# Two attention layers and a mixture of experts: the last token tile taken first, dispatch from slot numbers, combine weights by ScalarE, combine by halves

## The reference

```python
x = x + xattn(layernorm(x), ctx, ctx, mask, ...)      # 16 heads, softmax over 257 context rows
x = x + attn(layernorm(x), W_Q, W_K, W_V, W_O)        # 16 heads, rotary angles, causal, 32 tokens
# mixture of experts on xn = layernorm(x) as 8 groups (G) of 128 tokens (S), 8 experts (E), C = 32
logits = einsum('GSM,ME->GSE', xn, router_w)
raw = softmax(logits); idx1 = argmax(raw); gate1 = raw at idx1; idx2, gate2: the same without idx1
p1 = place of the token in the queue of expert idx1; p2 = place in that of idx2, behind all first choices
combine[g,s,e,c] = gate1*(e==idx1)*(c==p1)*(p1<C) + gate2*(e==idx2)*(c==p2)*(p2<C)
dispatch = (combine != 0)
expert_inputs = einsum('GSEC,GSM->EGCM', dispatch, xn)
hidden = gelu(expert_inputs @ w0) * (expert_inputs @ w1)          # width 1368
out = einsum('EGCM,GSEC->GSM', hidden @ wo, combine)
x = x + out
```

## Time and profile before

| | us |
|---|---|
| median of 3 runs | 539.1 (538.63 to 541.59) |
| the profiled execution's own time | 542.8 |
| its span, first to last instruction | 541.0 |
| TensorE busy | 495.8 (92%) |
| VectorE busy | 394.0 (73%) |
| ScalarE busy | 324.6 (60%) |
| GpSimd busy | 256.6 (47%) |

### The profile page before, as it was taken

The page is one execution under the profiler, slowest core; times in us unless marked ns, Lnnn a source line. Parts: engine busy times, 40 slices in busy tenths (PEclk is TensorE's granted clock), DMA queues, the critical chain, the costliest instruction groups (busy, mean ns, idle before and its releaser), DMA issues.

```text
span 541.0 us, 18283 instructions
## 1 busy us (share of the span) xinstructions
PE 495.8 (92%) x6637; PEld 456.4 (84%) x6637; DVE 394.0 (73%) x1007; ACT 324.6 (60%) x839; POOL 256.6 (47%) x343
## 2 busy tenths in 40 slices
PE   1898999998999999999996578999999999999996
...
DVE  2545555676676667677687867789999999999963
...
PEclk9979999999999999999997665899999999999998
...
GB/s 171 187 74 88 26 42 40 43 42 23 42 22 39 39 28 31 39 39 2 3 5 310 3 1 1 118 197 154 162 231 176 188 145 197 171 160 217 80 1 78
DMA packets 58126, 48.92 MB, mean 90 GB/s; under 512 B 20942, under 2 KB 49744, under 8 KB 58064
## 3 DMA queue, kind: packets, MB, share of 16 engines
...
HBM read 46.86 MB, written 1.08 MB: 89 GB/s over the span
## 4 chain that ended last, share of the span: by engine, by line
PE 81%; issue 6%; ACT 4%; DVE 3%; DMA 3%; SPq 1%; POOL 1%; ACTq 0%; DVEq 0%; POOLq 0%
PE bank L225 20%; PE bank L227 18%; PE bank L226 18%; PE bank L638 5%; PE bank L606 3%; PE bank L659 3%; PE bank L563 2%; ACT Pr L1094 2%; PE bank L1024 2%; DMA w_raw<-in_L_xattn_Wk 2%; PE bank L913 2%; PE bank L795 1%; DMA last_prob<-Pr 1%; PE bank L766 1%; PE bank L755 1%
## 5 line engine op out<-in xcount | busy, mean ns | idle before, releaser
L225 PE MATMUL bank<-XT_lo,W_hi 128*128 128x256 f32 (+1 forms) x352 | 100.5, 286 | 1.4 <-ACT XT_lo L1282 1.4
L226 PE MATMUL bank<-XT_hi,W_lo 128*128 128x256 f32 (+1 forms) x352 | 100.1, 284 | 0.0
L227 PE MATMUL bank<-XT_hi,W_hi 128*128 128x256 f32 (+1 forms) x352 | 99.8, 284 | 0.0
L2275 POOL TENSOR_TENSOR W_lo<-raw,W_hi 128x256 fp32r<-128x256 f32 (+1 forms) x88 | 87.7, 996 | 7.0
L2190 POOL TENSOR_TENSOR Pr<-Pr,rinv 128x1028 f32<-128x1028 f32 (+2 forms) x32 | 60.5, 1890 | 49.6 <-DVE rinv L1441 48.9
L1094 ACT ACTIVATE Pr<-Sc,nmax 128x257 f32<-128x257 f32 x128 | 63.8, 501 | 22.2 <-DVE nmax L1430 19.5
L1430 DVE CUSTOM_DVE_ANT_0 Sc<-bank,mask_add 128x257 f32<-128x257 f32 x128 | 47.0, 423 | 40.0 <-PE bank L606 17.3
L1922 DVE TENSOR_TENSOR W_lo<-raw,W_hi 128x512 fp32r<-128x512 f32 (+1 forms) x88 | 69.4, 789 | 4.6 <-ACT W_hi L1261 1.1
L2116 DVE TENSOR_TENSOR hid_lo<-hid,hid_hi 128x256 fp32r<-128x256 f32 (+1 forms) x88 | 71.6, 814 | 1.5 <-ACT hid_hi L1337 1.5
L2273 POOL CAST W_hi<-raw 128x256 fp32r<-128x256 f32 (+1 forms) x88 | 39.9, 453 | 63.3 <-PE bank L227 37.4
L225 PEld LDWEIGHTS bank<-XT_lo,W_hi 128*128 128x128 f32 (+1 forms) x352 | 66.5, 189 | 1.7 <-issue 1.7
...
## 6 DMA issues: line engine op xcount, KB each, us to landing
...
last_prob<-Pr SPq DMA_DIRECT2D x128, 1.0 KB, 1.8
...
```

The costliest lines, as they stand in the source:

```text
L225: pe.matmul(dst, a_hi, b_lo, start=first, stop=False)
L226: pe.matmul(dst, a_lo, b_hi, start=False, stop=False)
L227: return pe.matmul(dst, a_hi, b_hi, start=False, stop=last)
L2275: po.tensor_tensor(W2_lo[0:w, m % RW, :], raw2[0:w, t, :], f(W2_hi[0:w, m % RW, :]), ALU.subtract)\
```

## The change

- The tail's order is rewritten on all engines so that tile 7's steps come as soon as they can; the routing of early tiles is moved behind them.
- `disp` has a buffer per tile and is made from the slots (`past`, a token's slot number, or one beyond all slots where its place is over 32): by VectorE in two instructions for tiles 2, 4, 5, 6, 7, by GpSimd in three for tiles 0, 1, 3. The last tile's `XT_lo` is copied by VectorE, its `XT_hi` by ScalarE.
- `C_all` is no longer made in the tail. In steps 6 to 21 of the expert stage ScalarE makes one half of a tile's weights with two ACTIVATEs: `far = |past - slot|`, then `relu(gate - gate*far)`. GpSimd adds the two halves of a tile at steps 12, 14, ... 26, and the four `turn_weights_of` come at steps 26, 28, 30 and 48.
- At the end the combine matmuls of experts 0 to 3 for four tiles stand around the last `down`; the tiles go in the order 0, 2, 4, 6, 1, 3, 5, 7, with a semaphore after half of `keep_expert`; the sum goes into `x_sb`, so no buffer is waited for.

```diff
-    disp = sb("disp", [P, 2, E * CAP], F32R, early)
+    disp = sb("disp", [P, TT, E * CAP], F32R, early)
+    BY_POOL = (0, 1, 3)
+    WEIGH_AT = 6
+    TURN_AT = [26, 28, 30, 48]
+    MERGE = [0, 2, 4, 6, 1, 3, 5, 7]
+    MERGE_BANK = [6, 1, 4, 2, 5, 0, 3, 7]
...
         def turn_weights_of(i):
             pe.wait_ge(sm["r_weighed"], 2 * i + 2)
+            for by in ("y_read_act", "y_read_dve"):
+                pe.wait_ge(sm[by], 3 if i < 3 else 5)
...
         up(*place(0))
         up(*place(1))
-        turn_weights_of(TT // 2 - 1)
         for m in range(ALL):
             up(*place(m + 2))
+            if m in TURN_AT:
+                turn_weights_of(TURN_AT.index(m))
+            if m == ALL - 1:
+                pe.wait_ge(sm["ct_read"], TT // 2)
+                pe.wait_ge(sm["y_read_act"], E)
+                pe.wait_ge(sm["y_read_dve"], E)
+                combine(0, 0)
+                pe.wait_ge(sm["h_done"], done(*place(ALL - 3)))
             down(*place(m))
+        combine(1, 0)
+        pe.wait_ge(sm["h_done"], done(*place(ALL - 2)))
+        combine(2, 0)
+        combine(3, 0)
+        pe.wait_ge(sm["y_part_act"], 1)
+        combine(0, 1)
+        pe.wait_ge(sm["y_part_dve"], 1)
+        combine(1, 1)
+        combine(2, 1)
+        combine(3, 1)
...
+        for j in range(4, TT):
+            combine(j, 0)
+            combine(j, 1)
...
+        def weigh(t, c):                              # ScalarE
+            ac.wait_ge(sm["tail_left"], 2)
+            if t + c > 0:
+                ac.wait_ge(sm["w_act"], 4 * t + 2 * c)
+            ac.activation(far[:, :], slot_no, ACT.Abs, bias=past[:, c, one(t)], scale=-1.0).then_inc(sm["w_act"], 1)
+            ac.wait_ge(sm["w_act"], 4 * t + 2 * c + 1)
+            if c == 1 and t > 0:
+                ac.wait_ge(sm["r_weighed"], t)
+            ac.activation((C_all[:, t, :], second_of[:, :])[c], far[:, :], ACT.Relu, bias=gate[:, c, one(t)],
+                          scale=less_gate[:, c, one(t)]).then_inc(sm["w_act"], 1)
...
             ac.activation(hid_hi[0:w, m % RW, :], hid[0:w, m % RH, :], ACT.Copy).then_inc(sm["hhi_done"], 1)
-            if m == 0:
-                keep_weights_of(TT // 2 - 1)
+            if WEIGH_AT <= m < WEIGH_AT + 2 * TT:
+                weigh(*divmod(m - WEIGH_AT, 2))
+            if m - 1 in TURN_AT:
+                keep_weights_of(TURN_AT.index(m - 1))
...
         def disperse(t):                              # VectorE
-            ve.wait_ge(sm["r_weighed"], t + 1)
-            if t >= 2:
-                ve.wait_ge(sm["r_x_made"], t - 1)
-            ve.tensor_scalar(disp[:, t % 2, :], C_all[:, t, :], 0.0, None, ALU.not_equal).then_inc(sm["r_disp"], 1)
+            if t < EARLY:
+                ve.wait_ge(sm["r_reach"], 1)
+            else:
+                need(("reach", t))
+            mark(("disp0", t), ve.tensor_scalar(disp[:, t, :], slot_no, past[:, 0, one(t)], None, ALU.is_equal))
+            need(("disp0", t))
+            ve.scalar_tensor_tensor(out=disp[:, t, :], in0=slot_no, scalar=past[:, 1, one(t)], in1=f(disp[:, t, :]),
+                                    op0=ALU.is_equal, op1=ALU.add).then_inc(sm["d_disp"], 1)
...
-            if j >= 4:
-                ve.wait_ge(sm["out_done"], 16 * 4)
-            ve.tensor_tensor(fin[:, j % 4, :], bk[j][:, 0:D], x_sb[:, j, :], ALU.add).then_inc(sm["fin_done"], 1)
+            ve.tensor_tensor(x_sb[:, MERGE[j], :], bk[MERGE_BANK[j]][:, 0:D], x_sb[:, MERGE[j], :], ALU.add)\
+              .then_inc(sm["fin_done"], 1)
...
+        def disperse(t):                              # GpSimd, tiles 0, 1 and 3
+            po.tensor_scalar(second[:, :], slot_no, past[:, 1, one(t)], None, ALU.is_equal).then_inc(sm["r_disp"], 1)
+            po.tensor_scalar(disp[:, t, :], slot_no, past[:, 0, one(t)], None, ALU.is_equal).then_inc(sm["r_disp"], 1)
+            po.wait_ge(sm["r_disp"], n + 2)
+            po.tensor_tensor(disp[:, t, :], f(disp[:, t, :]), second[:, :], ALU.add).then_inc(sm["r_disp"], 1)
+
+        def add_weights(t):
+            po.wait_ge(sm["w_act"], 4 * t + 4)
+            po.tensor_tensor(C_all[:, t, :], C_all[:, t, :], second_of[:, :], ALU.add).then_inc(sm["r_weighed"], 1)
```

More of the change, by code:

```diff
@@ L297, in values_at @@
         return bk[7] if isinstance(t, int) and t == TT - 1 else front(t)
+    BY_POOL = (0, 1, 3)
+    BY_DVE = [t for t in range(TT) if t not in BY_POOL]
     def inputs_of(t):
@@ L1009, in down, with combine @@
             last.then_inc(sm["y_made"], 1)
+        def combine(j, k):
+            t = MERGE[j]
+            last = pe.matmul(bk[MERGE_BANK[j]][:, 0:D], CT[:, t, k, :], Y[:, t, k, :], start=k == 0, stop=k == 1)
+            if k == 1:
+                last.then_inc(sm["comb_made"], 1)
         pe.sem_inc(sm["y_made"], 1)
```

304 lines of the change are left out of this document (135 added, 169 removed).

## The result

The changed kernel takes 532.99 us (median of 4 runs, 531.39 to 534.27); the kernel before, run beside it, 540.22 (4 runs, 538.63 to 541.59). The ratio is 0.9866, with a 95% interval from 0.9822 to 0.991: 7.2 us faster, where 7.4 were predicted and the time given was 531.7. In a second group of runs it was 533.5 (9 runs) against 538.75 (23 runs), ratio 0.9912 (0.9876 to 0.9948): by it 4.7 us, within 2.8 and 6.7.

A forecast was written before the change was run, and what follows sets the result against it. TensorE was taken to bound the expert stage; in the tail no engine is full and TensorE stands behind waits in its list. Tail -7.8, end -4.3, transpositions +1.2, stall +3.5 sum to -7.4: 539.1 to 531.7 us, range 528 to 536.

The forecast's parts named there:

- The tail up to the output projection: Tail: reordered steps bring tile 7's norm 1.7 us earlier, scaled scores 2.0, turned weights 6.9, output projection 8.2.
- From there to the last dispatch matrix: Tail, output projection to dispatch matrix 7: 13.92 us before, stays at 14, matrix 7 comes 8.0 earlier.
- It loses about 1.3: Tail: tile 7's normalisation on VectorE waits about 1.3 us behind a step needing tile 6's exp on ScalarE.
- GpSimd's compares: Tail: three instructions of 0.73 us per GpSimd dispatch matrix, matrices 0 and 1 in 4.4 us, hidden.
- ScalarE's stall: Expert stage: two ACTIVATEs cost 1.05 us together, step 2.27 instead of 2.14; stall 3.5 us, from 0 to 4.3.
- Transpositions: Expert stage: three more transpositions of combine weights on a full TensorE, 0.4 us each, +1.2.
- The end: Last down to span's end: combine matmuls moved early, TensorE busy at 2.4 GHz, no buffer wait; 4.3 us less, bounds 3 and 4.7.
- Carrying the difference to the median: Profiled execution lies 3.7 us above the runs' median; the -7.4 is applied to that median: 539.1 to 531.7.
- The clock did not fall in the stall: Rival, expert stage: stall at step 13 or 14 drops TensorE's clock, 534.1 to 536.5 us; chance 0.15.
- VectorE was not the late one: Rival, expert stage: GpSimd's eight adds hold VectorE, 3.8 us more, 532.5 to 535.5; chance 0.10.
- No compare took 2 us: Rival, tail: GpSimd's compares take 2 us each, tail gains 4 less, 535.7 us; chance 0.05.
- ScalarE did stall TensorE: Rival, expert stage: ACTIVATE pair costs 0.92 us or less or TensorE's lead suffices, no stall, 528.2 us; chance 0.13.

The follow-up runs named there:

- e8: Changed kernel with four moves in TensorE's tail list undone: 539.73 us, ratio 1.0011 to the kernel before.
- e6: Changed kernel with combine weights formed by VectorE in the tail, not by ScalarE and GpSimd in the expert stage: 537.33 us, ratio 0.9981 to the kernel before.
- e10: Changed kernel with dispatch matrices of tiles 0, 1 and 3 formed by VectorE instead of GpSimd: 534.73 us, ratio 0.9927 to the kernel before.
- e2: Changed kernel with all 16 combine matmuls behind both last copies to Y, none early: 534.05 us, ratio 0.9913 to the kernel before.
- e12: Changed kernel with one move undone, tile 7's positions behind dispatch 5 on TensorE: 532.99 us, ratio 0.9891 to the kernel before.
- e4: Changed kernel with the same 32 ACTIVATEs spread one a step over steps 3 to 34, GpSimd's adds later: 528.8 us, ratio 0.9827 to the kernel before.
- e1: Kernel before with the new end alone: 535.9 us, ratio 0.9941 to the kernel before.
- e3: Changed kernel without ScalarE's 32 ACTIVATEs, combine weights zero, GpSimd's adds kept: 529.91 us, ratio 0.985 to the kernel before.

## Why the prediction was right, and where it was not

The sum came out (7.4 for 7.2), but that is in part luck: two misses are in it that cancel, and against the second group's 4.7 it would have been 2.7 too much.

- **The tail up to the output projection** was right in each step. From qk's transposition, before and after: tile 7's norm turned 1.6 earlier (predicted 1.7), scaled scores 1.9 (2.0), weights ready 5.1 (5.4), weights turned 6.7 (6.9), output projection 8.3 (8.2). e8 says that the order on TensorE carries this, and e6 that the order is worth little without VectorE being relieved: undone alone they give back 7.4 and 8.0 of 9.8. They are not two terms to be added; whichever is missing holds the chain. In both traces the clock was also lower (0.57 and 0.64 over the tail, 0.70 in after), so the sizes hold less firmly than the order.
- **From there to the last dispatch matrix** I said 14, and it was 12.4. The step that failed is "It loses about 1.3": tile 7's norm waited 0.21 for tile 6's exp. Then I took 7.8 instead of the 8.4 that the layout gave, because the old list, laid out the same way, came out short. Measured, the tail is 9.8 shorter, so the term was 2 us too small: about 1.1 for this wait, and about 1 for the clock, which I had not counted in the tail at all (8.8 at nearly the same clock).
- **GpSimd's compares** take 0.92 to 1.41 and not 0.73, and TensorE waits 0.63 and 0.52 for matrices 1 and 3. Nearly hidden, as said. On VectorE they cost 2.9 in e10's trace.
- **ScalarE's stall**: 3.4 for 3.5. The step was 2.21 (2.27), the wait for the add 1.51 (1.2), the copy of expert 0 1.17 (1.18). It came at step 14 in one piece of 1.48 us, as foreseen, and again at step 24, 0.68, which I had not foreseen and which e2 and e12 lack (stage 4.6 instead of 5.1). The two ACTIVATEs last 0.49 and 0.60, and the second starts 0.53 behind the first and the gelu 0.50 behind the second, so the pair costs 1.03: my 1.05, and above the 0.92 at which it would be free. The row by which the Trainium skill ("ScalarE: Activation LUTs", section "Rules for kernel authors") would leave such work to VectorE names relu, and not abs as the prediction has it. Here it would not have paid: on VectorE the weights lengthened the tail by 8.0 us (e6), and 32 ACTIVATEs at one a step cost nothing (e4).
- **Transpositions**: 0.44 a group for 0.4. Four groups stand in the stage, not three more: before, the fourth stood behind `up(1)` and so in the cold start.
- **The end**: 4.3 for 4.3, in the profiled executions. The reason is half shown, and about 1.6 of it are had only where the clock would fall. I wrote that the clock should stay up if TensorE stays busy; it does (e1 and all others), but e2 kept it up while idle too.
- **Carrying the difference to the median** failed: "It lies 3.7 above the median of the runs, and the difference is carried to that". The profiled execution was of the old kernel's low-clock group. By the traces' means the parts add up to -9.8 - 0.4 (cold start) + 5.1 - 4.3 = -9.4, while the runs say -7.2 and -4.7. Both traces of before are of its low-clock group, and the two of after are among its three shortest of 13 executions (531.39 and 531.26, of 531.25 to 536.57). Of a high-clock execution of the old tail there is one trace, e1's (0.968): 56.05 from qk to the fourth gelu, where the two of before have 59.9 and 59.2 and the new tail 48.1, so 7.9 of gain instead of 11 to 12. With the stage's 5.1 lost and the end's 4.3 gained that is 7.1; why the high-clock median lies only 3.0 above after's it does not settle.
- **Rivals.** The clock did not fall in the stall (1.00 in all windows). VectorE was not the late one (e3). No compare took 2 us. ScalarE did stall TensorE. The Trainium skill ("SBUF — State Buffer", section "SBUF: two separate sides") would have GpSimd and a VectorE instruction with two SBUF inputs exclude each other: the low parts (`hid_lo`) took 0.95 us where their neighbours took 0.42, as before, but the eight adds cost the stage nothing.
